# Pairing the dense products of an audio tower and rewriting every engine's order around the pairs

## The reference, cut to what matters

```python
off = einsum('bwkc,ock->bow', xr, w_off) + b_off      # dy, dx for each of 46 windows x 16 taps
px = base + dx;  wy = max(0, 1 - |dy|)
val = wy * ((1 - frac) * x[floor(px)] + frac * x[floor(px) + 1])
tok = concat(cls, einsum('bckw,dck->bwd', val, w_def) + b_def) + positions      # 47 x 128
h = tok + attention(layernorm(tok))     # one head, plus tanh(hq + hk + b1) @ W2 on every pair of tokens
out = h + moe(layernorm(h))             # 8 experts, the best 2 by a gate, and a shared expert
```

## Time and profile before

| | |
|---|---|
| median of 3 runs | 1146.52 us (1141.79 to 1148.27) |
| profiled execution | 1144.36 us |
| its span, first to last instruction | 1142.5 us |
| TensorE matmuls busy | 1047.9 us (92%) |
| ScalarE busy | 914.3 us (80%) |
| VectorE busy | 682.8 us (60%) |
| share of the last chain | PE 62%, ACT 26%, issue 5%, DMA 4%, DVE 2% |
| mean granted TensorE clock | 0.972 |

### The profile page before, as it was taken

One profiled execution on the slowest core, in us unless ns is written; L12 is line 12 of the kernel. 1 busy time (PEld: TensorE's weight loads), 2 busy tenths in 40 slices (PEclk: granted clock), 3 DMA queues, 4 the chain that ended last, 5 costly groups with the idle time before them and its releaser, 6 DMA issues.

```text
span 1142.5 us, 16775 instructions
## 1 busy us (share of the span) xinstructions
PE 1047.9 (92%) x6214; PEld 489.0 (43%) x6214; DVE 682.8 (60%) x1293; ACT 914.3 (80%) x1431; POOL 2.0 (0%) x11
## 2 busy tenths in 40 slices
PE   3478878899999999999999999999999999999977
PEld 0234334344534444443444444344444535444544
DVE  2354546576575666666576666657566765756544
ACT  3596979798797979889797979979797997979333
POOL 0000000000000000000000000000000000000000
PEclk7698899999999999999999999999999999999989
DMA  7744243623535373443626343452635244330122
GB/s 247 253 149 147 87 162 114 225 96 124 182 116 181 107 226 115 137 154 117 213 75 230 113 160 129 143 202 78 213 112 191 104 137 147 107 126 5 64 67 68
DMA packets 63009, 160.56 MB, mean 141 GB/s; under 512 B 21456, under 2 KB 40144, under 8 KB 60624
## 3 DMA queue, kind: packets, MB, share of 16 engines
q1 hardware_dynamic: 62640, 159.18, 41.9%
q10 hardware_dynamic: 288, 0.32, 0.1%
HBM read 154.26 MB, written 5.21 MB: 140 GB/s over the span
## 4 chain that ended last, share of the span: by engine, by line
PE 62%; ACT 26%; issue 5%; DMA 4%; DVE 2%; SPq 1%; ACTq 0%; DVEq 0%
PE bank L645 28%; ACT HT L342 21%; PE bank L770 8%; PE bank L611 7%; PE bank L758 5%; PE bank L623 2%; PE bank L681 2%; PE bank L740 2%; PE bank L661 2%; DMA c_mats<-in_mats 1%; PE bank L777 1%; ACT TH L362 1%; PE bank L630 1%; PE bank L722 1%; PE bank L688 1%
## 5 line engine op out<-in xcount | busy, mean ns | idle before, releaser
L342 ACT ACTIVATE HT<-PXB,c_near 128x736 f32<-128x736 f32 x768 | 696.8, 983 | 55.5 <-PE bank L645 54.4
L645 PE MATMUL bank<-HT,XN 128*64 128x368 f32 x3072 | 540.1, 489 | 24.1 <-DVE HT L486 23.2
L486 DVE TENSOR_SCALAR HT<-HT 128x2208 f32<-128x2208 f32 x256 | 329.7, 1302 | 25.8 <-ACT HT L342 25.8
L645 PEld LDWEIGHTS bank<-HT,XN 128*64 128x64 f32 x3072 | 207.1, 139 | 316.5 <-issue 271.6
L578 DVE TENSOR_TENSOR GE<-HE,CB 128x376 f32<-128x376 f32 x128 | 69.6, 547 | 150.7 <-ACT HE L411 141.4
L758 PE MATMUL bank<-Z,c_experts 128*128 128x376 f32 x288 | 121.9, 506 | 0.0
L770 PE MATMUL bank<-GE,c_experts 128*128 128x376 f32 x256 | 106.9, 509 | 5.8 <-DVE GE L578 5.8
L411 ACT ACTIVATE HE<-bank,c_mats 128x376 f32<-128x376 f32 x128 | 72.7, 568 | 23.5 <-PE bank L758 23.1
L496 DVE SCALAR_TENSOR_TENSOR VT<-bank,WYB 128x368 f32<-128x368 f32 x128 | 68.5, 535 | 34.9 <-PE bank L645 34.8
L611 PE MATMUL bank<-VT,c_mats 128*128 128x368 f32 x256 | 83.3, 478 | 0.0
L349 ACT ACTIVATE SQHC<-bank 128x376 f32<-128x376 f32 x16 | 7.7, 484 | 80.6 <-PE bank L661 80.6
(11 more groups left out here) (101 smaller groups left out, 672.5 us busy)
## 6 DMA issues: line engine op xcount, KB each, us to landing
PXB<-pw SPq DMA_DIRECT2D x64, 768.0 KB, 5.9
XT<-in_turned SPq DMA_DIRECT2D x16, 1536.0 KB, 10.5
XN<-in_x SPq DMA_DIRECT2D x64, 384.0 KB, 3.9
WYB<-pw SPq DMA_DIRECT2D x128, 192.0 KB, 5.6
CB<-shares SPq DMA_DIRECT2D x32, 752.0 KB, 4.2
out<-OUTS SPq DMA_DIRECT2D x16, 188.0 KB, 7.3
c_experts<-in_experts SPq DMA_DIRECT2D x1, 1152.0 KB, 19.0
c_mats<-in_mats SPq DMA_DIRECT2D x1, 1134.5 KB, 16.7
```

The costliest lines, as they stand in the source:

```text
L342: act.activation(HT[k % HTS][:, c, :, :].rearrange("p g (n w) -> p g n w", n=4), src, ACT.Abs, bias=cs["lneg"][:, 3 * half + c:3 * half + ...
L486: dve.tensor_scalar(rows_, rows_, 1.0, 0.0, ALU.subtract, ALU.min).then_inc(hat_ready, 1)
L645: mm = pe.matmul(bank[b % 2][64 * g:64 * g + 64, 0:2 * HW], XN[b // 2][:, b % 2, C * ch:C * ch + C], HT[k % HTS][:, c, 2 * g:2 * g + 2, :] ...
```

## The change

The dense pieces of TensorE stand in pairs, both halves of a sequence behind one another, so that a unit has eight runs of dense work and eight gaps for all else instead of sixteen. The lists of ScalarE and VectorE are rewritten to go with it. `n1` joins `n0` in being run a step early, and so does `j3` on VectorE; `m0` moves on TensorE and ScalarE from the end of a step to the start of the next. VectorE's constants move into `b3` of unit 0. No instruction is added or removed, and SyncE's list is as it was.

```diff
 SHIFTED = {
-    "tensor": {"n0": 2, "m0": 1},
-    "vector": {"d8": -3, "r6": 0, "j0": 2, "j1": 2, "j2": 2},
-    "scalar": {"m0": 1, "r6": 0, "k0": 2, "k1": 2, "k2": 2, "k3": 2},
+    "tensor": {"n0": 2, "n1": 2},
+    "vector": {"d8": -3, "r6": 0, "j0": 2, "j1": 2, "j2": 2, "j3": 2},
+    "scalar": {"r6": 0, "k0": 2, "k1": 2, "k2": 2, "k3": 2},
     "sync": {"d9": -3},
 }
 ORDER = {
-    "tensor": ("fs n1 m1 r7 f0 n2 r8 ds n3 d8 m2 n4 r9 f1 n5 m3 n6 r10 m4 n7 f2 n8 d0 m5 n9 m51 f3 n10 m52 d1 n11 r11 f4 "
-               "n12 d2 f5 n13 r12 d3 n14 f6 n15 d4 a3 f7 d5 a4 n0 b3 d6 d7 m0").split(),
-    "scalar": ("k4 fs k5 r7 f0 k6 k7 k8 r9 f1 k9 m3 k10 m41 m4 k11 f2 k12 k13 m5 m51 f3 k14 m52 k15 f4 k0 f5 k1 r12 k2 f6 "
-               "k3 a3 f7 a4 r6 m0").split(),
-    "vector": ("r7 d8 j3 o0 m1 j4 r8 j5 m2 o1 j6 g0 g1 j7 m3 o2 j8 r10 m4 j9 o3 g2 j10 j11 o4 g3 j12 j13 r11 o5 g4 j14 j15 "
-               "g5 o6 r12 j0 r13 r14 g6 o7 j1 a4 r6 g7 j2 b3").split(),
+    "tensor": ("fs m0 r7 f0 m1 n2 n3 r8 ds d8 m2 r9 f1 n4 n5 m3 r10 m4 f2 d0 n6 n7 m5 m51 f3 d1 n8 n9 m52 r11 f4 d2 n10 n11 "
+               "f5 r12 d3 f6 n12 n13 d4 f7 d5 n14 n15 a3 d6 d7 n0 n1 a4 b3").split(),
+    "scalar": ("fs m0 k4 r7 f0 k5 k6 r9 f1 k7 m3 m41 k8 m4 f2 k9 m5 k10 m51 f3 k11 m52 k12 f4 k13 f5 k14 r12 f6 k15 k0 f7 k1 "
+               "a3 k2 r6 k3 a4").split(),
+    "vector": ("r7 d8 o0 m1 j4 j5 r8 o1 m2 g0 j6 j7 m3 o2 r10 m4 g1 j8 j9 o3 g2 j10 j11 o4 g3 r11 j12 j13 o5 g4 r12 j14 r13 "
+               "r14 j15 g5 o6 g6 j0 j1 o7 g7 j2 r6 a4 j3 b3").split(),
     "sync": ("d9 l0 l1 e0 e1 e2 l2 w0 p0 l3 x0").split(),
 }
...
             def b3(m, h):
 
+                if 2 * m + h == 0:
+                    constants()
                 dve.wait_ge(tok_full, 2 * m + h + 1)
...
             steps("vector", pieces, -3, -1)
-            dve.wait_ge(const_in, 16)
-            dve.tensor_scalar(pe_b[:, :], cs["peT"][:, :], cs["bdef"][:, 0:1], None, ALU.add).then_inc(dve_consts, 1)
-            dve.tensor_tensor(cls_pe[:, :], cs["cls"][:, :], cs["peT"][:, 0:1], ALU.add).then_inc(dve_consts, 1)
-            dve.wait_ge(dve_consts, 2)
-            chain(dve.tensor_scalar(least[:, :], cs["tri"][:, :], -TINY, TINY, ALU.mult, ALU.add))
-            for p in range(2):
-                chain(dve.tensor_copy(h0[p][:, :, 0:1], cls_pe[:, :].unsqueeze(1).broadcast_to([128, NB, 1])))
             dve.wait_ge(zeroed, 7)
```

More of the change, by code:

```diff
@@ L67 @@
     -3: {**ORDER, "sync": ("x0 p0").split()},
-    -2: {**ORDER, "scalar": ("a3 a4 k0 k1 k2 k3").split(), "vector": ("a4 j0 j1 j2").split(),
+    -2: {**ORDER, "tensor": ("a3 a4 n0 n1").split(), "scalar": ("a3 a4 k0 k1 k2 k3").split(),
+         "vector": ("a4 j0 j1 j2 j3").split(),
          "sync": ("l0 x0 l1 l2 l3 p0").split()},
@@ L498, in dense_out, with constants @@
                 return piece
+            def constants():
+                dve.wait_ge(const_in, 16)
+                dve.tensor_scalar(pe_b[:, :], cs["peT"][:, :], cs["bdef"][:, 0:1], None, ALU.add).then_inc(dve_consts, 1)
+                dve.tensor_tensor(cls_pe[:, :], cs["cls"][:, :], cs["peT"][:, 0:1], ALU.add).then_inc(dve_consts, 1)
+                dve.wait_ge(dve_consts, 2)
+                chain(dve.tensor_scalar(least[:, :], cs["tri"][:, :], -TINY, TINY, ALU.mult, ALU.add))
+                for p in range(2):
+                    chain(dve.tensor_copy(h0[p][:, :, 0:1], cls_pe[:, :].unsqueeze(1).broadcast_to([128, NB, 1])))
             def b3(m, h):
+                if 2 * m + h == 0:
+                    constants()
                 dve.wait_ge(tok_full, 2 * m + h + 1)
```

## The result

The changed kernel takes 1152.11 us (median of 6 runs, 1150.36 to 1153.03) against 1144.95 for the kernel before, run beside it: a ratio of 1.0052, 95% interval 1.003 to 1.0073 (the two medians alone would give 1.0063). It is slower by 0.5%. The forecast was 1134 and faster, with a range up to 1149. The profiled execution has a span of 1149.7 us, 7.2 more than before.

What follows compares the result with a forecast made beforehand. TensorE's list was taken to bound steady units, 66.1 us against 65.9 before, so the gain was the start's 17.7 us. Start, steps and tail gave 1118 us; 15 for clock falls made 1133, put at 1134, range 1104 to 1149.

Steps and rivals of the forecast that it cites:

- the term for the clock: TensorE's clock falls behind the `d5` stall in about two of three units, 1.6 to 1.8 us each: 15 us.
- What pairing saves: TensorE's list: eight fewer dense runs save 1.1 to 2.7 us a unit, taken as 2.2, leaving 62.3 us of work.
- Stretch (1): Steady unit, TensorE from the start of `m0` to the end of `m4`: 18.1 us, only `r9` close to a wait.
- Stretch (2): From the end of `m4` to `d5`, which waits for VectorE's `g5`: 29.3 us, TensorE idle 2.9 of it.
- From `d5` to the end of `a3`: TensorE's expert product, dense pair and `a3` behind the stall: 0.63 + 3.86 + 1.43 us at full clock.
- Stretch (3): From the end of `a3` to the next `m0`, through ScalarE and VectorE: 12.9 us, TensorE waiting 0.9 at `m0`.
- The start: Moved constants and new orders bring `m0` of unit 0 from 99.42 to 81.7 us: 17.7 gained.
- that cover: `c_mats` lands by 47.5 us, well before `b3`, hiding its wait; otherwise 12 of the start's 17.7 us stay lost.
- their terms at full clock: The sum's entries for single steps without clock falls: step 1 at 59.9 us, steps 2 to 12 at 66.1 each.
- The rival that the clock falls in nearly every unit: Full-price falls at the `d5` stall, 13 x 2.7 = 35 us, giving 1153; chance 0.10 slower, 0.10 for 1140 to 1150.
- The rule: Skill text: a loop with an idle gap between matmul bursts pays on every turn; 13 x 1.7 = 22 us, 1142 in all.

Runs made afterwards that it cites:

- the two filling runs: Changed kernel with eleven unread 128-column products on TensorE just ahead of `d5`, once with start on, once with it off: 1134.66 and 1133.27 us.

## Why the prediction was wrong

The step that failed is the term for the clock. The pairs, the three stretches and the start came out near what was laid out:

- **What pairing saves** was right: 2.2 us forecast for the list, 62.3 us of work; with all waits but 0.18 gone the unit is 62.48, and split pairs cost 2.46 us of work again.
- **Stretch (1)**, `m0` to the end of `m4`: 630.16 - 611.80 = 18.4 for 18.1. `r9` came as close to a wait as counted, on the other side of it (0.16 us).
- **Stretch (2)**, to the start of `d5`: 659.28 - 630.16 = 29.1 for 29.3, with TensorE idle for 2.86 (forecast 2.9), released by VectorE's `g5`. Laying out three in-order lists by hand from rows of the old trace gave it to 0.2 us.
- **From `d5` to the end of `a3`**: 7.76 for 5.92. 1.64 of the difference is the clock, which the forecast held in a term of its own; 0.20 the pieces themselves (4.69 + 1.43 = 6.12).
- **Stretch (3)**: 679.98 - 667.04 = 12.94 for 12.9, the wait at `m0` 1.14 for 0.9.
- **The start**: 82.55 for 81.7. `c_mats` was covered, and `j3` free, as forecast. The forecast priced that cover at 12 us; with the constants put back it is 10.4 at `m0` of unit 0 (92.96 - 82.55).
- **The clock is the step that failed**, "I take it that the clock falls in about two of three units". It fell behind 12 of the 13 stalls, and in steps 1 and 2 behind the wait ahead of `m0` as well (3.40 and 2.63 us). Its price of "about 1.6 to 1.8" was right, 1.64. So it cost 12 x 1.64 = 19.7 in the stalls at `d5`. Steps 1 and 2 were 3.1 and 2.7 us longer than their terms at full clock, and I put that down to their falls (the slow pairs alone are 6.63 - 3.93 = 2.7 and 5.57 - 3.93 = 1.6 us, the slow products ahead of them come on top); no run takes these two falls away alone. Together it is 25 where the sum had 15. I had counted no stall that long in those two steps.
- **The rest of the miss is in small terms.** At full clock the unit would be 68.18 - 1.64 = 66.54 and not 66.1, which the two filling runs confirm with 66.57 and 66.55. That is 0.44 x 11 = 4.8 us, steps 13 and 14 are about 1 longer each besides the clock, and start and step 0 are 1.0 longer: 7.8 together. 25 - 15 + 7.8 = 18, which is the difference of 1152 and 1134.
- **The chances.** The rival that the clock falls in nearly every unit is what happened, but it needed 2.5 us a unit to end slower, by my count. It got there with 1.64 and 0.44, since the margin of the forecast without the clock (26 us) was itself thinner by the small terms, and since steps 1 and 2 paid too. That this rival's 1153 lies so near the 1152 measured is luck: it had 13 falls at 2.7 us. Errors of 0.1 to 0.2 us in a stretch are good readings and still 2 to 5 us of a total that repeats them; here all but one had the same sign.
- **The rule.** The Trainium skill, "TensorE: Matmul & The Clock Gate" (HAM oscillation), has a loop with a gap pay on every turn; the waits of its example are longer, about 3 to 5 us. The trace of the changed kernel agrees nearly, with gaps of 2.81 to 2.88 us: 12 of 13 turns, 1.64 us each. The run with `b3` early agrees less, 6 of 13. By the rule I had worked out 1142; with the small terms it would have been 1150. I gave more weight to one stretch of 2.20 us behind which nothing happened than to the nearness of 2.9 to 3.15, and took the middle. The trace of before had more to say than the row that I took: between 80 and 220 us it has five idle stretches of 3.15 to 5.99 us, and TensorE was slow behind all five.

## What to carry to other kernels

Before moving pieces between in-order lists, lay out the lists of all engines beside each other, and where a piece ends up waiting look at what stands directly ahead of its producer: here one swap of two neighbours on VectorE was worth 36 us of 1150, and three pieces moved turned a loss of 0.5% into a gain of 6.7%. An idle stretch of TensorE near 3 us is to be priced at its own length and at the slower work behind it, on every turn of the loop; here that came true for 12 of 13 turns in one order and 6 of 13 in another, and at 1.6 us the second part was nearly gone. A change that is good in one part (start, pairs) can read as no change in the total, so its parts are worth timing alone.

## What the runs showed of the hardware that was not expected

- A fall of the clock came behind idle stretches of TensorE much shorter than the 3.15 us of before, but not behind all of one length:

| idle | where | run | clock fell behind |
|---|---|---|---|
| 2.81 to 2.88 us | `d5` | changed kernel | 12 of 13 |
| 2.79 to 2.87 | `d5` | the same with the constants back | 12 of 13 |
| 2.82 to 2.90 | `d5` | `b3` early | 6 of 13 |
| 1.57 to 1.66 | `d5` | `g5` ahead of `j15` | 0 of 13 |
| 1.57 to 1.64 | `d7` | `g5` ahead of the gate | 1 of 11 |
| 1.02 to 1.03 | `r7` | `b3` early | 2 of 12 |

- The length alone does not decide it. Two pairs of waits show it best. The kernel before has 3.15 us ahead of `m52` at 194.19, and the clock fell; with only the constants moved the same wait is 3.16 at 184.54, and the pieces behind it ran at full speed (2.08 us for a dense piece, 3.93 for two). And at the start of step 0 TensorE waits 0.73 and 0.57 us in the changed kernel and just as long with `g5` ahead of `j15`; the pair behind took 3.93 us in the first (84.78) and 5.62 in the second (84.11), with a granted clock of 0.57 from 84 to 88. What else decides was not settled.
- The moment at which the clock fell moved from unit to unit. In the changed kernel the expert product behind the stall took 1.62 us at 318.36, 1.26 at 659.28 and 0.95 at 1000.29, and the pair behind it 4.83, 5.21 and 5.52: the lower clock began a little later in each unit, while the whole stretch from `d5` to `a3` stayed at 6.31 to 6.33. The price per fall at `d5` hardly moved in any run, 1.62 to 1.70 us.
- Useless work can pay: eleven products of 128 columns, 2.6 us of filling a unit, took 17.5 and 18.8 us off the changed kernel.
